# Second convolution of a graph network: the last two chunks' share of the scores taken from weights times attention rows, and half a chunk of work held back

## What is computed

```python
def gat_conv(x, src, dst, W, a_src, a_dst, b, heads, out_ch):
    h = (x @ W).reshape(n, heads, out_ch)
    alpha_src = jnp.einsum('nhc,hc->nh', h, a_src)
    alpha_dst = jnp.einsum('nhc,hc->nh', h, a_dst)
    e = jax.nn.leaky_relu(alpha_src[src] + alpha_dst[dst], NEG_SLOPE)
    ...                       # softmax of e over the edges into each node
    out = segment_sum(h[src] * alpha[:, :, None], dst)
    return out.reshape(n, heads * out_ch) + b
...
h = gat_conv(x, src, dst, W1, a_src1, a_dst1, b1, 8, 768)
h = jax.nn.elu(h)
out = gat_conv(h, src, dst, W2, a_src2, a_dst2, b2, 1, 768)   # "conv2" below
...
x = _layernorm(x + out)       # then the second network
```

## Time and profile before

| | |
|---|---|
| median of 3 runs | 358.46 us (358.44 to 358.57) |
| the profiled execution, its own time | 358.43 us |
| its span in the trace | 356.6 us |
| TensorE busy with matmuls | 347.9 us (98%) |
| ScalarE / VectorE / GpSimd busy | 218.5 / 213.4 / 242.4 us |
| mean share of the DMA queue that loads the weights | 47.0% of 16 engines |

### The profile page before, as it was taken

The page is one execution under the profiler, slowest core; times in us unless marked ns, Lnnn a source line. Parts: engine busy times, 40 slices in busy tenths (PEclk is TensorE's granted clock), DMA queues, the critical chain, the costliest instruction groups (busy, mean ns, idle before and its releaser), DMA issues.

```text
span 356.6 us, 6079 instructions
## 1 busy us (share of the span) xinstructions
PE 347.9 (98%) x2058; PEld 298.9 (84%) x2060; DVE 213.4 (60%) x545; ACT 218.5 (61%) x376; POOL 242.4 (68%) x163
## 2 busy tenths in 40 slices
PE   7999999999999999999999999999999999999994
PEld 4888889889888988988898898898667888788883
DVE  4999883263546418244552732636687897944776
ACT  5987697547737754864674575476376866255601
POOL 2379769657693884968569396674257898687911
PEclk9999999999999999999999999999999999999999
DMA  7987969576656556656574754757072656246002
GB/s 235 312 299 225 391 214 257 179 240 144 227 150 203 176 155 205 170 176 183 170 217 143 224 170 141 246 159 237 11 218 94 217 179 198 99 135 221 0 2 88
DMA packets 24544, 65.15 MB, mean 183 GB/s; under 512 B 1952, under 2 KB 3024, under 8 KB 24528
## 3 DMA queue, kind: packets, MB, share of 16 engines
q1 hardware_dynamic: 20864, 55.02, 47.0%
q10 hardware_dynamic: 3664, 9.92, 10.8%
HBM read 64.15 MB, written 0.79 MB: 182 GB/s over the span
## 4 chain that ended last, share of the span: by engine, by line
PE 92%; DVE 4%; ACT 1%; DMA 1%; issue 1%; DVEq 0%; SPq 0%
PE ps L1008 64%; PE ps L1298 10%; PE ps L1096 9%; PE ps L1130 2%; PE ps L1362 2%; PE ps L1075 1%; DMA x_sb<-in_x 1%; PE ps L1060 1%; PE ps L1192 1%; DVE stats L1744 1%; DVE ps L1964 1%; DVE z L1971 1%; PE ps L1157 0%; PE ps L1383 0%; PE ps L1310 0%
## 5 line engine op out<-in xcount | busy, mean ns | idle before, releaser
L370 POOL TENSOR_TENSOR ring_lo<-raw,ring_hi 128x768 fp32r<-128x768 f32 x92 | 167.0, 1849 | 70.9 <-ACT ring_hi L357 70.8
L357 ACT ACTIVATE ring_hi<-raw 128x768 fp32r<-128x768 f32 x96 | 77.3, 839 | 35.7 <-PE ps L1008 28.8
L386 POOL TENSOR_TENSOR ring_lo<-raw,ring_hi 128x512 fp32r<-128x512 f32 (+1 forms) x40 | 59.5, 1517 | 20.3 <-ACT ring_hi L379 20.2
L1008 PE MATMUL ps<-ring_hi,zT_hi 128*128 128x256 f32 (+1 forms) x256 | 69.3, 345 | 0.4 <-ACT zT_hi L808 0.4
L1008 PE MATMUL ps<-ring_lo,zT_hi 128*128 128x256 f32 (+1 forms) x256 | 67.1, 337 | 0.0
L1008 PE MATMUL ps<-ring_hi,zT_lo 128*128 128x256 f32 (+1 forms) x256 | 66.8, 338 | 0.0
L1515 DVE CUSTOM_DVE_ANT_0 e<-ps,att 128x768 f32<-128x768 f32 x38 | 34.3, 953 | 47.6 <-PE ps L1008 47.6
L1008 PE MATMUL ps<-ring_hi,xT_hi 128*128 128x512 f32 x192 | 51.2, 343 | 0.3 <-ACT xT_hi L702 0.3
L1008 PE MATMUL ps<-ring_lo,xT_hi 128*128 128x512 f32 x192 | 50.0, 336 | 0.0
L1008 PE MATMUL ps<-ring_hi,xT_lo 128*128 128x512 f32 x192 | 49.8, 337 | 0.0
L1008 PEld LDWEIGHTS ps<-ring_lo,zT_hi 128*128 128x128 f32 x256 | 43.0, 188 | 5.6
(11 more groups left out here) (172 smaller groups left out, 545.4 us busy)
## 6 DMA issues: line engine op xcount, KB each, us to landing
raw<-in_L_gnn_W SPq DMA_DIRECT2D x54, 768.0 KB, 4.5
raw<-in_L_gnn_Wr SPq DMA_DIRECT2D x8, 768.0 KB, 4.3
att<-in_L_gnn_a_src ACTq DMA_DIRECT2D x10, 384.0 KB, 4.0
att<-in_L_gnn_a_dst ACTq DMA_DIRECT2D x10, 384.0 KB, 5.2
raw<-in_L_gnn_W SPq DMA_DIRECT2D x4, 384.0 KB, 5.0
x_sb<-in_x SPq DMA_DIRECT2D x3, 256.0 KB, 4.8
rows_hc<-in_L_gnn_b SPq DMA_DIRECT2D x1, 512.0 KB, 7.6
rows_hc<-in_L_gnn_g SPq DMA_DIRECT2D x1, 512.0 KB, 8.4
```

The costliest lines, as they stand in the source:

```text
L357: eng.activation(slot_hi(c), raw_chunk(c), ACT.Copy).then_inc(hi_done, 1)
L370: eng.tensor_tensor(slot_lo(c), raw_chunk(c), slot_hi(c).bitcast(F32), ALU.subtract)\
L386: eng.tensor_tensor(ring_lo[:, q["ring_at"]:q["ring_at"] + w], raw[:, q["raw_group"], q["raw_at"]:q["raw_at"] + w], ring_hi[:, q["ring_at" ...
L1008: last = pe.matmul(ps[:, at + to:at + to + hi - lo], a, b[:, lo:hi], start=start and n == 0 and to != D, stop=stop and n == PASSES - 1, sk ...
```

## The change

Conv2's score of a node is a sum over input channels, z · W2 · a. For the last two chunks of head 7 (chunks 4 and 5, called LATE) the product is now taken in the other order: GpSimd multiplies the raw rows of W2 with the attention rows (`weigh_rows`, four products of 128x768), ScalarE sums each along the row (`row_sum`, a Copy with a sum as second output), and TensorE multiplies the resulting 128x4 numbers `attw` with zT (`late_rows`, six matmuls) and turns the two rows into columns (`late_columns`). VectorE adds these to the dots of the columns that hold only chunks 0 to 3 (`ends`). Only the 512-column piece of tile 1 keeps its place in the dots with chunks 0 to 3 added in. The main products of chunks 4 and 5 then stand around and behind the scores, in place of the matmuls on zeros. The attention rows are loaded a second time, before the last phase's weights (`att2`, in the place of `hs`). The low parts of two bias rows go from VectorE to GpSimd. Head 7 leaves the loops of TensorE and GpSimd: its half of the chunk before (`held_back`, tile 1 of chunk 5) follows `aggregate_T`. The aggregation of conv2 is written for waits part by part (`aggregate_conv2`), and ScalarE splits conv2's tile 1 in two pieces, after the softmax weights.

```diff
@@ SyncE, before the last phase's loads
+            sp.wait_ge(unpacked, 2)
+            for n, v in enumerate((b0_as2, b0_ad2)):
+                sp.dma_start(att2[:, n * D:(n + 1) * D], v[0:1, :].partition_broadcast(P)).then_inc(att2_loaded, 16)
             load_phase(PHASES - 1, w2_of(H0 - 1))
@@ GpSimd
-            with pool.Fori(1, H0) as h:
+            with pool.Fori(1, H0 - 1) as h:
                 head(h)
+            def weigh_rows(c):
+                for half_at in range(2):
+                    m = 2 * LATE.index(c) + half_at
+                    if m >= 2:
+                        pool.wait_ge(attw_done, m - 1)
+                    pool.tensor_tensor(weighted_row(m), raw_chunk(c), att2[:, half_at * D:(half_at + 1) * D], ALU.mult)\
+                        .then_inc(weighted_done, 1)
+            phase_lo(PHASES - 2)
+            pool.wait_ge(raw_full[LATE[0] // 2], 16 * PHASES)
+            pool.wait_ge(att2_loaded, 32)
+            weigh_rows(LATE[0])
+            for c in range(LATE[0]):
+                split_lo(pool, PHASES - 1, c)
+            weigh_rows(LATE[1])
+            split_lo(pool, PHASES - 1, LATE[0])
+            pool.wait_ge(attw_hi_done, 1)
+            pool.tensor_tensor(attw_lo[:, :], attw[:, :], attw_hi[:, :].bitcast(F32), ALU.subtract).then_inc(attw_lo_done, 1)
+            split_lo(pool, PHASES - 1, LATE[1])
...
@@ ScalarE
+                if last:
+                    after_exps(h, between=lambda: (row_sum(0), row_sum(1)))
+                    elu(h, between=lambda: (split_hi(act, PHASES - 1, LATE[1]), row_sum(2)))
+                    row_sum(3)
+            def row_sum(m):
+                act.wait_ge(weighted_done, m + 1)
+                act.activation(weighted_row(m), weighted_row(m), ACT.Copy, scale=SLOPE - 1.0 if m % 2 else 1.0,
+                               accum_out=attw[:, m:m + 1]).then_inc(attw_done, 1)
...
+            act.wait_ge(zv_rows_ps, 1)
+            act.activation(zv_rows[:, :], ps[0:2, ZV_AT:ZV_AT + N], ACT.Copy).then_inc(zv_rows_done, 1)
             chunks_hi(0, 2)
             leaks(A_CONV2)
-            projected_tile_hi(A_CONV2, 1)
+            chunks_hi(2, 3)
             exps(A_CONV2, (0, 1))
-            chunks_hi(2, 3)
+            act.wait_ge(tile0_done, 1)
+            projected_tile_hi(A_CONV2, 0)
+            weights_tiles_hi(A_CONV2)
+            act.wait_ge(chunk_used, CH * PHASES)
+            for done, cols in ((h_hi_part, slice(N, D)), (h_hi_done, slice(0, N))):
+                if done is h_hi_done:
+                    act.wait_ge(h_lo0_done, before(A_CONV2) + 1)
+                act.activation(feat(h_hi, A_CONV2, 1)[:, cols], source_at(A_CONV2, 1)[:, cols], ACT.Copy).then_inc(done, 1)
@@ TensorE
-                    accumulate(2 * h, h - 1, c)
+                    accumulate(2 * h, h - 1, c, tiles=(0,) if held_back and c == CH - 1 else range(NT))
                 aggregate_T(h)
+                if held_back:
+                    accumulate(2 * h, h - 1, CH - 1, tiles=(1,))
...
+            for c in range(LATE[0]):
+                last = last_accumulate(c, 1, piece=0)
+            last.then_inc(early_bank_done, 1)
...
+            for c in range(LATE[0]):
+                if c == 2:
+                    late_rows()
+                if c == 3:
+                    late_columns()
+                last_accumulate(c, 1, piece=1).then_inc(chunk_used, 1)
+            pe.wait_ge(partial_done, 2)
+            for c in LATE:
+                chunk(PHASES - 1, c)
+                if c == LATE[1]:
+                    last_accumulate(c, 0, piece=0, passes=(0,))
+                    scores(A_CONV2)
+                    last_accumulate(c, 0, piece=0, passes=(1, 2))
+                else:
+                    last_accumulate(c, 0, piece=0)
...
+            for c in LATE:
+                last_accumulate(c, 0, piece=1)
+                last = last_accumulate(c, 1, piece=0)
+            last.then_inc(tile0_done, 1)
+            pe.wait_ge(a_dst_done, before(A_CONV2) + 2)
+            for c in LATE:
+                last_accumulate(c, 1, piece=1).then_inc(chunk_used, 1)
...
-            scores(A_CONV2)
-            keep_warm(12, idle)
             weights_tiles(A_CONV2)
-            aggregate(A_CONV2)
+            aggregate_conv2()
@@ VectorE
-            tile_dots(A_CONV2, 0)
-            conv2_lo(0)
-            dve.wait_ge(wide_piece_done, 1)
-            piece_dots(slice(N, D), None, (partial_done, partial_done))
-            projected(A_CONV2, 1)
-            dve.wait_ge(partial_done, 2)
-            piece_dots(slice(0, N), partial, (a_src_done, a_dst_done))
+            piece_dots(0, slice(0, BANK), None, ...)
+            piece_dots(0, slice(BANK, D), partial[:, 4:6], ...)
+            piece_dots(1, slice(0, N), None, ...)
+            dve.wait_ge(zv_ps, 1)
+            dve.tensor_tensor(ends[:, :], ps[:, ZV_COLS_AT:ZV_COLS_AT + 4], partial[:, 0:4], ALU.add).then_inc(zv_added, 1)
+            dve.wait_ge(chunk_used, CH * (PHASES - 1) + LATE[0])
+            piece_dots(1, slice(N, D), ends[:, 2:4], ...)
             masked_scores(A_CONV2)
             weigh(A_CONV2, 0)
             weigh(A_CONV2, 1)
-            conv2_lo(1)
+            conv2_lo(0)
             weights_tiles_lo(A_CONV2)
             inverse_sums(A_CONV2)
+            conv2_lo(1)
```

More of the change, by code:

```diff
@@ L179, in build_gnn @@
         minus_mean = sb("minus_mean", [P, NT])
-        partial = sb("partial", [P, 2])
+        partial = sb("partial", [P, 6])
+        ends = sb("ends", [P, 4])
+        attw = sb("attw", [P, 4])
+        attw_hi = sb("attw_hi", [P, 4], F32R)
+        attw_lo = sb("attw_lo", [P, 4], F32R)
+        zv_rows = sb("zv_rows", [2, N])
         half = sb("half", [P, 1])
@@ L464, in masked_at, with src_col, dst_col @@
             return ps[:, at:at + N]
+        def src_col(a, k, j):
+            if isinstance(a, int) and a == A_CONV2 and j == 0:
+                return ends[:, 0:1]
+            return a_s[:, pair(a, k, j)]
+        def dst_col(a, k, i):
+            if isinstance(a, int) and a == A_CONV2 and i == 0:
+                return ends[:, 1:2]
+            return a_d[:, pair(a, k, i)]
         def small(a):
@@ L829, in after_exps @@
                 weights_hi(h)
-                for c in (4, 5):
+                if between is not None:
+                    between()
+                for c in (4,) if between is not None else (4, 5):
                     split_hi(act, 2 * h + 1, c)
@@ L1037, in project_chunk, with accumulate @@
                 last.then_inc(chunk_used, 1)
-            def accumulate(p, h, c):
+            def accumulate(p, h, c, tiles=range(NT)):
                 if c % 2 == 0:
                     pe.wait_ge(z_lo_done, 3 * h + c // 2 + 1)
-                chunk(p, c)
-                for i in range(NT):
+                if tiles[0] == 0:
+                    chunk(p, c)
+                for i in tiles:
                     last = product(ACC, i, node_tile(zT_hi, c, i), node_tile(zT_lo, c, i),
                                    slot_hi(c), slot_lo(c), False, False)
-                last.then_inc(chunk_used, 1)
+                if tiles[-1] == NT - 1:
+                    last.then_inc(chunk_used, 1)
             def scores(a):
@@ L1139, in aggregate @@
                             part(j, pT_lo, h_hi, False, False)
[L1140 to L1141 removed]
                         last = part(1, pT_hi, h_lo, False, True)
[L1143 to L1146 removed]
+                    last.then_inc(nat_done, 1)
             pe.wait_ge(zeros_set, 1)
@@ L1261, in _ @@
-            for c in range(CH):
-                last = last_accumulate(c, 1, piece=1)
-            last.then_inc(wide_piece_done, 1)
-            pe.wait_ge(h_lo0_done, before(A_CONV2) + 1)
-            for c in range(CH):
-                last_accumulate(c, 1, piece=0).then_inc(chunk_used, 1)
-            pe.wait_ge(z_lo_done, 3 * H0)
-            idle = PROJ + BANK
-            scores(A_CONV2)
-            keep_warm(12, idle)
+            pe.wait_ge(z_hi_done, 3 * (H0 - 1) + 2)
+            for c in (2, 3):
+                chunk(PHASES - 1, c)
+                last_accumulate(c, 0, passes=FIRST_TWO)
@@ new lines, in _, with late_rows @@
+            pe.wait_ge(z_lo_done, 3 * (H0 - 1) + 2)
+            for c in (2, 3):
+                last = last_accumulate(c, 0, passes=LAST_ONE)
+            last.then_inc(early_bank_done, 1)
+            for c in range(LATE[0]):
+                last = last_accumulate(c, 1, piece=0)
+            last.then_inc(early_bank_done, 1)
+            def late_rows():
+                pe.wait_ge(z_lo_done, 3 * H0)
+                pe.wait_ge(attw_lo_done, 1)
+                for c in LATE:
+                    at = 2 * LATE.index(c)
+                    for n, (a, b) in enumerate(three(attw_hi[:, at:at + 2], attw_lo[:, at:at + 2],
+                                                     zT_hi[:, c, :], zT_lo[:, c, :])):
```

(39 more changed lines are left out.)

109 lines of the change are left out of this document (65 added, 44 removed).

## The result

The changed kernel takes **356.92 us** (median of 5 runs, 356.62 to 357.08), the kernel before in the same comparison 358.57 (5 runs, 358.44 to 358.74). The ratio is 0.995, with a 95% interval of 0.9938 to 0.9963: faster by 1.3 to 2.2 us. A second comparison of the same two kernels gave 356.98 and 0.9947 (0.993 to 0.9965), 1.3 to 2.5 us. The forecast was 356.4, in a range of 355.3 to 357.7. The profiled execution took 356.69 us.

What follows compares the result with a forecast made beforehand. TensorE was taken as the bound, with some 4 us of hole at the seam set by the softmax chain; 3.25 - 0.6 - 0.45 - 0.1 = 2.1 us gained gave 356.4 us, range 355.3 to 357.7 (8 in 10).

Steps and rivals of the forecast that it cites:

- What bounds the kernel: Whole kernel: TensorE holds 92% of the chain that ended last; only its waits or needless work can be won.
- The hole: Seam between phase 15's products and conv2's aggregation: some 4 us set by the softmax chain, which real products could fill.
- Step 1: Held-back half and row sums: ELU 0.3 to 0.6 us earlier, phase 15 starts 0.4 us earlier (0 to 0.55).
- Step 2: Phase 15's start to the softmax weights' transposes: 0.2 us wait at late_rows, transposes at 256.45 instead of 259.70, 3.25 earlier.
- the rival: GpSimd's product dearer than its subtraction: gain of 2.1 us gone at 0.5 us more per product; chance 0.06.
- Step 3: Aggregation and behind it: 0.6 us given back by waits for splits, 0.45 before the second network, 0.1 for hand-overs.
- the two places that were named: Aggregation: TensorE waits 0.25 us for VectorE's low part of tile 0's features, 0.35 for its last low part, tile 1.
- Edits costed at nothing: Bias rows on GpSimd (1.25 us each, in its idle time), second copy of attention rows, later loads, unrolled head 7: free.
- Sum: Whole kernel: 3.25 - 0.6 - 0.45 - 0.1 = 2.1 us gained, giving 356.4 us.
- Rivals: More given back, 357.7 (0.18); nothing moves, 358.2 to 358.7 (0.06); GpSimd's product dearer (0.06); clock falls, 360.7 (0.02).
- all its signs: Phase 15 about 242.1, late_rows near 249.6, transposes near 256.5 and 262.6, two aggregation waits of 0.2 to 0.4, products 1.8 us.
- the reason against the clock: Against a falling clock (0.02): longest foreseen TensorE idle is 0.6 us, and over 0.6 us without matmul it stayed 1.00.

Runs made afterwards that it cites:

- the last two experiments: Changed kernel with VectorE's last low part in two pieces, each waited for apart: 356.23 us; changed kernel with tile 0's products reading h_hi for h_lo: 356.72 us.

## Why the prediction was right, step by step

**What bounds the kernel**: right. The hole was the thing to be won, and the waits behind it stayed small.

**Step 1**: the mechanism is right, the size was at its upper bound. ScalarE's rows of the changed kernel:

```profile
236.59 0.84 ACT L902 ACTIVATE am<-am 128x768 f32<-128x768 f32 x1
237.32 0.19 ACT L902 ACTIVATION_READ_ACCUMULATOR am<-am 128x1 f32 x1
237.41 0.84 ACT L902 ACTIVATE am<-am 128x768 f32<-128x768 f32 x1
```

A row sum costs an instruction of its own of 0.19 us, which starts ahead of the end of the copy: 0.82 us from sum to sum (237.41 - 236.59) for 0.76 for a copy, 0.06 more where nothing to 0.15 was allowed. The ELU starts at 238.97, that is 3.52 us behind the weight transposes for 4.17 before: 0.65 earlier, for 0.3 to 0.6 in the forecast. Phase 15 starts at 242.30, 6.85 behind them for 7.40: a gain of 0.55, where 0.4 was taken.

**Step 2**: right in the mechanism and nearly in size. GpSimd's row is what it rests on:

```profile
232.81 3.65 POOL L682 TENSOR_TENSOR am<-raw,hs 128x768 f32<-128x768 f32 x2 [4.21 <-DMA raw<-in_L_gnn_W]
236.43 7.29 POOL L394 TENSOR_TENSOR ring_lo<-raw,ring_hi 128x768 fp32r<-128x768 f32 x4
243.69 3.65 POOL L682 TENSOR_TENSOR am<-raw,hs 128x768 f32<-128x768 f32 x2
247.30 1.86 POOL L394 TENSOR_TENSOR ring_lo<-raw,ring_hi 128x768 fp32r<-128x768 f32 x1
249.11 0.20 POOL L694 TENSOR_TENSOR attw_lo<-attw,attw_hi 128x4 fp32r<-128x4 f32 x1
...
251.20 1.28 POOL L702 TENSOR_TENSOR zT_hi<-rows_hc,zT_hi 1x512 fp32r<-1x512 f32 x1
```

A product takes what a subtraction takes (3.65 for two), the small subtraction 0.20 us, a 1x512 row 1.28. `attw_lo` was done at 249.31 and `late_rows` starts at 249.46, which is the hand-over of 0.15 us found above: a wait of 0.09 us, where 0.2 was counted. That this meeting is the weak place was right too: the kernels with longer products lose nearly all that is added, and at 0.56 us more for each the gain is gone, as the rival put it (0.5). The transposes of the weights came at 256.64; less the 0.29 us by which this profile runs late, that is 256.35, for 256.45. TensorE's own path in the forecast ended at 256.35; the 0.15 us more of step 1 and the 0.1 less of waiting should have made that 256.1. TensorE is busy for 3.96 of the 4 us from 253 to 257, so the work up to there is some 0.25 us longer than counted. Some of it shows around the tiny transposes: those of the scores start 0.43 us behind the product before them (253.07 - 252.64), for 0.23 by the width.

**Step 3**: right in kind, and right in size as a sum. TensorE's rows in the aggregation:

```profile
256.64 0.75 PE L1178 MATMUL ps<-ident,e 128*128 128x128 f32 x4
257.49 0.61 PE L1402 MATMUL ps<-h_hi,pT_hi 128*128 128x512 f32 x2
258.21 0.63 PE L1402 MATMUL ps<-h_lo,pT_hi 128*128 128x512 f32 x2
...
259.80 0.62 PE L1402 MATMUL ps<-h_lo,pT_hi 128*128 128x512 f32 x2
```

Pairs otherwise follow each other at 0.35 us. From 257.49 to 258.21 it is 0.72, and ahead of 259.80 it is 0.42: waits of 0.37 and 0.07 us at the two places that were named, where 0.25 and 0.35 were counted. The pair behind each wait takes 0.46 and 0.45 us, 0.1 more than the others, which the forecast did not have; with that, the 24 matmuls take 4.88 us (to 262.37), for 4.85. The first product stands 0.85 us behind the transposes, for 1.0, and from it to the transposes of the second network's input it takes 262.69 - 257.49 = 5.20 us, for the 5.10 of the forecast. So 3.35 - 2.57 = 0.78 us are given back up to there, 0.85 were counted. What the step didn't say, and the last two experiments showed: VectorE has two jobs in a row here, and taking the first wait away lets the second one show after 0.18 us.

**Edits costed at nothing**: for the bias rows this held alone and here, and the argument that the place decides stands. What the step did not see is the other side: on VectorE, ahead of its dots, they would have cost 5.6 us: they wait there for ScalarE's high parts, they take 2.4 us longer now that GpSimd is no longer idle beside them, and TensorE's clock falls. The rule of the Trainium skill, GPSIMD Engine Reference, section 3.1, was weighed against this edit. On the instruction by itself the rows agree with it (1.28 us on GpSimd, 0.68 on VectorE beside an idle GpSimd); for the kernel's time it points the wrong way here. The second copy of the attention rows cost nothing, as forecast: it is issued at 215.7 and 216.7 and lands within 5.8 us, and it is needed at 232.8. (The forecast's "up to 6.6 us" for the later loads is 6.8 by its own two numbers; the measured end of the last low part is 251.11.)

**Sum**: the seam gave 2.51 us for 2.1. Of that, 0.1 was won at the transposes of the weights, and 0.84 instead of 1.15 were given back behind them: between the input's transposes and the second network only 0.06 us were lost (1.35 for 1.29), where 0.3 were counted for a late low part and hand-overs. The second network's passes then lose 0.13 (3.20 for 3.07 us), and at VectorE's last instruction, 115.86 us behind the weight transposes for 118.22, 2.36 are left. The two profiled executions differ by 1.74 us: 0.29 of the 2.36 is lost ahead of head 7's weight transposes, 0.17 between VectorE's last instruction and the end of the span, and 0.16 outside the span. The medians moved by 1.65 and 1.78 us; the intervals (1.3 to 2.5 us over both comparisons) hold the trace's value too. The profiles of this study reach head 7 at times up to 0.9 us apart, so whether the 0.29 is more than chance isn't settled. That 2.1 lies as near to the medians as it does is in part luck: the seam gave 0.4 more than the sum, and what is lost outside it took as much and more away again.

**Rivals**: the forecast came in; all its signs are in the trace except that the second wait in the aggregation is 0.07 us and not 0.2 to 0.4. The step that was argued badly is the reason against the clock. That the clock stayed 1.00 over 0.6 us without a matmul says nothing of 1.9 or 3.1 us, and the price given for it (4.3 us, the whole aggregation doubled) is too high: in the traces without the zeros, and with the longer products, the low clock cost 1.1 to 1.25 us, for the aggregation took 5.43 us and not twice 4.43, and the clock was back in the window from 264. With the bias rows on VectorE it was low for longer and cost 2.0. What the prediction says of the products that replace the zeros fits the kernel before: take the zeros away and put nothing there, and the clock falls.

## What to carry to other kernels

Where TensorE waits for a chain of small steps on other engines, give it products that don't need that chain, and count what these products need from other engines: here GpSimd's row and TensorE meet within 0.1 us, and four products that are 0.56 us longer each cost the whole gain. When work is moved onto an engine that was idle, look at who ran beside its idle time: here a neighbour's two-input instructions took up to three times as long. Compare stretches from a point that the change doesn't reach, not start times of two traces.

## What was not expected of the hardware

- TensorE's granted clock stays 1.00 while the engine stands, and falls when it works again or up to 1.3 us later: behind 3.1 us of idle time in the profile without the zeros (all six runs have a mean of 0.989 to 0.992), behind 1.9 us in a profile with longer products (two runs of 11 have that mean, only one of the 11 has a trace). It cost 1.1 to 1.25 us in these profiles, and 2.0 where it stayed at 0.50 from about 255.0 to 261.9 us.
- VectorE's 1x512 subtraction of two SBUF rows: 0.68 us with GpSimd idle, 2.03 and 1.75 with GpSimd busy.
- On GpSimd one row of 512 columns takes 1.28 us, as 128 rows do (2.51 / 2); 128x4 takes 0.20.
- Matmuls with two columns of weights over 256 columns follow each other at 0.11 us (249.46 to 250.03 for five steps), those with 128 at 0.12: hardly faster.
- GpSimd's end of a small subtraction to TensorE's first matmul on it takes 0.15 us, in three kernels where TensorE stands waiting for it.
